# Queries and keys by halves of the heads in the first phase, and one plus the scale multiplied by GpSimd

## What is computed

```python
mod = (silu(c) @ wmod).reshape(2, 6, 1, 256)         # sa, ca, ga, sb, cb, gb
h  = layernorm(x) * (1 + ca) + sa                     # x: 2 x 2048 tokens x 256
xn = layernorm(h) * ln_g + ln_b
q, k, v = (xn @ W.T, in 8 heads of 32, for W in Wq, Wk, Wv)
def apply_rope(x):                                    # on q and k; x1, x2: a head's first and last 16
    return x * cos + concatenate([-x2, x1]) * sin
qp = einsum('bhtd,hd->bht', q[..., :3], head_dirs)    # and kp from k
```

## Time and profile before

| | us |
|---|---|
| Median of 3 runs | 2733.17 (2731.45 to 2739.83) |
| Profiled execution | 2730.83 |
| Its span, first to last instruction | 2729.1 |
| Part of the span in the changed phase | from about 23 to about 226 |

### The profile page before, as it was taken

One profiled execution on the slowest core, in us unless ns is written; L12 is line 12 of the kernel. 1 busy time (PEld: TensorE's weight loads), 2 busy tenths in 40 slices (PEclk: granted clock), 3 DMA queues, 4 the chain that ended last, 5 costly groups with the idle time before them and its releaser, 6 DMA issues. The chain is left out here.

```text
span 2729.1 us, 45326 instructions
## 1 busy us (share of the span) xinstructions
PE 2551.3 (93%) x14104; PEld 1541.0 (56%) x14104; DVE 2171.9 (80%) x4588; ACT 1589.6 (58%) x3509; POOL 554.8 (20%) x404
## 2 busy tenths in 40 slices
PE   7998999999999999996999999799989999997998
PEld 3444333333333333344777777578767777775877
DVE  5988999999999999975888888555658887885665
ACT  3443666666767766653666666544446666664442
POOL 1111011011100111035333333100033333331000
PEclk8997999999999999998999999999989999998999
DMA  3344354545445445453000000220020000001121
GB/s 131 118 133 125 102 133 114 131 122 149 115 110 130 121 126 135 128 177 106 16 17 15 21 16 15 64 89 22 2 63 9 8 9 8 10 16 43 46 68 40
DMA packets 124741, 204.95 MB, mean 75 GB/s; under 512 B 22736, under 2 KB 71952, under 8 KB 121280
## 3 DMA queue, kind: packets, MB, share of 16 engines
q1 hardware_dynamic: 111856, 170.39, 22.2%
q0 software_dynamic: 8688, 21.27, 2.8%
q10 hardware_dynamic: 4080, 11.86, 1.2%
HBM read 125.44 MB, written 54.13 MB: 66 GB/s over the span
## 5 line engine op out<-in xcount | busy, mean ns | idle before, releaser
L1084 ACT ACTIVATE probs<-st_ps 128x512 f32<-128x512 f32 (+3 forms) x640 | 339.0, 530 | 298.7 <-PE st_ps L1013 164.3
L1137 DVE SCALAR_TENSOR_TENSOR geo_x<-geo_rows,kp_t 128x512 f32<-128x512 f32 (+3 forms) x640 | 436.9, 706 | 3.8 <-ACT probs L1086 3.7
L1116 DVE TENSOR_REDUCE chunk_max<-a_ps 128x1 f32<-128x512 f32 (+3 forms) x640 | 358.6, 601 | 37.1 <-PE a_ps L996 31.7
L1086 ACT ACTIVATE probs<-geo_x 128x512 f32<-128x512 f32 (+3 forms) x640 | 360.7, 564 | 12.8 <-DVE geo_x L1143 12.8
L1417 PE MATMUL local_in_ps<-w_local,local_ht 128*128 128x512 f32 x1152 | 321.7, 416 | 9.4 <-ACT local_sq L1559 5.3
L1578 ACT ACTIVATE local_probs<-local_s_ps,local_bias,local_inv 128x256 f32<-128x256 f32 x512 | 282.6, 563 | 13.8 <-DVE local_bias L1673 13.8
L1585 ACT ACTIVATE local_pt<-local_pt_ps 128x512 f32<-128x512 f32 x256 | 152.3, 596 | 209.0 <-PE local_pt_ps L1475 200.7
L1028 PE MATMUL o_ps<-probs,vx_first 128*33 128x512 f32 (+3 forms) x1280 | 274.0, 550 | 0.0
L1856 PE MATMUL ff_ag_ps<-ff_ht_parts,w 128*128 128x512 f32 (+1 forms) x1056 | 255.4, 400 | 17.5 <-DVE ff_gate L1965 9.3
L1028 PE MATMUL o_ps<-probs,vx_ 128*33 128x512 f32 (+3 forms) x1280 | 270.3, 544 | 0.0
L1669 DVE TENSOR_REDUCE local_top<-local_s_ps 128x4 f32<-128x1024 f32 x128 | 156.7, 1224 | 120.9 <-PE local_s_ps L1461 120.9
(11 more groups left out here) (197 smaller groups left out, 4216.9 us busy)
## 6 DMA issues: line engine op xcount, KB each, us to landing
geo_rows<-geo SPq DMA_DIRECT2D x64, 512.0 KB, 7.6
piece_lo<-in_pieces POOLq DMA_DIRECT2D x15, 768.0 KB, 5.7
weight_parts<-piece_hi SPq DMA_DIRECT2D x15, 768.0 KB, 3.4
weight_parts<-piece_lo SPq DMA_DIRECT2D x15, 768.0 KB, 6.0
raw<-out_t SPq DMA_DIRECT2D x128, 64.0 KB
shares_in<-shares SPq DMA_DIRECT2D x64, 128.0 KB, 4.9
q_first<-q_parts SPq DMA_DIRECT2D x24, 256.0 KB, 4.1
k_first<-k_parts SPq DMA_DIRECT2D x24, 256.0 KB, 6.3
```

Of the source, the lines that this page charges most:

```text
L1084: act.activation(probs[:, s % PSLOTS, 0, off:GTOK], st_ps[:, (b * NB + s) % STBANKS, off:GTOK], ACT.Exp).then_inc(q["st_used"], 1)
L1086: act.activation(probs[:, s % PSLOTS, 1, off:GTOK], geo_x[:, s % GSLOTS, off:GTOK], ACT.Exp).then_inc(q["probs_ready"], 1)
L1116: dve.reduce_max(chunk_max[:, it, c:c + 1], a_ps[:, n % ABANKS, 0:width], AX.X).then_inc(q["a_used"], 1)
L1137: ins = dve.scalar_tensor_tensor(out[:, off:GTOK], geo[:, 1, at], kp_t[:, j, ds(b, 1)].rearrange("p o -> p o"), geo[:, 0, at], ALU.add, AL ...
```

## The change

In words, part by part:

- The weight columns of queries and of keys are ordered by halves of the heads: first the first 16 columns of all 8 heads (128 columns), then the last 16 of all. Both terms of the rotary sum then exist already, and the products with rotated columns go. `w_qkv` has 3 x 256 columns for 5 x 256.
- There are two units for four: queries and keys. A unit's `qk_ps[:, u, half, :]` holds both halves. `rot_c` is one instruction of 1024 columns with the cosine repeated, `rot_s` two of 512 with the halves exchanged (the sign now in the scale factor), the sum, `hi` and `lo` one of 1024 each.
- The three coordinates of a head's direction lie all in the first half, so that a product with the directions is one matmul for two.
- The product with one plus the scale moves from DVE to POOL, for groups 1 to 7; on DVE a wait for it is left. POOL does it behind its offset of the first norm and ahead of `second_scale`, and so ahead of the next fetch.
- The order on DVE becomes `rotate(n, 0)`, wait, `rotate(n, 1)`, `low_part(n, 0)`, `shifted(n + 1)`, `low_part(n, 1)`; that on ACT both `hi`, both values, `normed`.
- SP stores the queries as soon as their `lo` is there and the keys after theirs. A store now takes 16 rows of each of 8 heads, 8 x 16 x 512, where it took 128 successive rows.

The core of the diff:

```diff
@@ SP: send
-                    sp.wait_ge(q["hi_done"], 4 * n + 4 + START)
-                    sp.wait_ge(q["lo_done"], 4 * n + 4 + START)
                     for r, store in enumerate((S.q_parts, S.k_parts)):
+                        sp.wait_ge(q["hi_done"], 2 * n + r + 1 + START)
+                        sp.wait_ge(q["lo_done"], 2 * n + r + 1 + START)
                         for part, tile in enumerate((hi, lo)):
                             for k in range(CC):
-                                dst = store[part, ds(n // GPB * H + k * 4, 4), :, ds(n % GPB * GTOK, GTOK)]
-                                sp.dma_start(dst.rearrange("h d t -> (h d) t"), tile[:, r, k, :].bitcast(F32)).then_inc(q["parts_out"], 16)
+                                dst = store[part, ds(n // GPB * H, H), k * HD:(k + 1) * HD, ds(n % GPB * GTOK, GTOK)]
+                                sp.dma_start(dst, tile[:, r, k, :].bitcast(F32)).then_inc(q["parts_out"], 16)
@@ POOL: the loop over n
                     pool.tensor_tensor(offset[:, 0, :], centre[:, 0, :], rstd[:, 0, :], ALU.mult).then_inc(q["rstd1"], 1)
+                    pool.wait_ge(q["x_used"], n + 1 + START)
+                    pool.tensor_tensor(xhat[:, :, :], xhat[:, :, :], S.mod[:, 1, ds(n // GPB, 1), :].to_broadcast([P, GT, C]), ALU.mult).then_inc(q["chain1"], 1)
                     second_scale(n)
@@ ACT: group
-                    for u in range(4):
-                        if u == 3 and more:
-                            normed(n + 1)
-                        act.wait_ge(q["rope_done"], 4 * n + u + 1 + START)
+                    for u in range(2):
+                        act.wait_ge(q["rope_done"], 2 * n + u + 1 + START)
...
-                        act.activation(hi[:, u // 2, u % 2, :], qk[:, u // 2, u % 2, :], ACT.Copy).then_inc(q["hi_done"], 1)
+                        act.activation(hi[:, u, :, :], qk[:, u, :, :], ACT.Copy).then_inc(q["hi_done"], 1)
+                    for u in range(2):
+                        act.wait_ge(q["v_ready"], 2 * n + u + 1 + START)
+                        act.activation(S.v[:, ds(n * GT + 2 * u, 2), :, :],
+                                       v_ps[:, u, :].rearrange("p (t h d) -> p t h d", t=2, h=H), ACT.Copy).then_inc(q["v_used"], 1)
+                    if more:
+                        normed(n + 1)
@@ PE: group
-                    for u in range(4):
-                        pe.wait_ge(q["qk_used"], 4 * n + u + 1 + START)
-                        for rot in range(2):
-                            c0 = (u // 2 * 2 + rot) * C + u % 2 * P
+                    for u in range(2):
+                        pe.wait_ge(q["qk_used"], 2 * n + u + 1 + START)
+                        for half in range(2):
+                            c0 = u * C + half * P
...
-                        for k in range(CC):
-                            last = pe.matmul(dot_ps[:, :], (dirs_q if u == 0 else dirs)[:, k, :], qk[:, u, k, :],
-                                             start=k == 0, stop=k == CC - 1)
-                        last.then_inc(q["dot_ready"], 1)
+                        pe.matmul(dot_ps[:, :], (dirs_q if u == 0 else dirs)[:, :], qk[:, u, 0, :], start=True, stop=True).then_inc(q["dot_ready"], 1)
@@ DVE: modulated, rotate, group
                     if not scaled:
-                        dve.wait_ge(q["x_used"], n + 1 + START)
+                        dve.wait_ge(q["chain1"], n * LINKS + 3 + START)
+                        return
...
+                    dve.wait_ge(q["qk_ready"], 2 * n + u + 1 + START)
+                    dve.wait_ge(q["rope_done"], 2 * n + u + START)
+                    dve.scalar_tensor_tensor(rot_c[:, :, :], qk_ps[:, u, :, :], sc, cos[:, here].rearrange("p (o t) -> p o t", o=1).to_broadcast([P, 2, GTOK]), ALU.mult, ALU.mult)
+                    dve.scalar_tensor_tensor(rot_s[:, 0, :], qk_ps[:, u, 1, :], -sc, sin[:, here], ALU.mult, ALU.mult)
+                    last = dve.scalar_tensor_tensor(rot_s[:, 1, :], qk_ps[:, u, 0, :], sc, sin[:, here], ALU.mult, ALU.mult)
...
-                    for u, piece in enumerate((modulated, shifted, None, None)):
-                        rotate(n, u)
-                        if u:
-                            low_part(n, u - 1)
-                        if more and piece:
-                            piece(n + 1)
...
+                    rotate(n, 0)
+                    if more:
+                        modulated(n + 1)
+                    else:
+                        gates(2)
+                    rotate(n, 1)
+                    low_part(n, 0)
+                    if more:
+                        shifted(n + 1)
+                    low_part(n, 1)
```

More of the change, by code:

```diff
@@ L26 @@
 BH = B * H
+HD = D // 2
 EPS = 1e-5
@@ L123, in __init__ @@
         sb, _, sem = allocators(nc, ctx, S.sems)
-        self.w = sb("w_qkv", [P, CC, 5 * C])
+        self.w = sb("w_qkv", [P, CC, 3 * C])
         self.cos, self.sin = sb("cos_t", [P, T]), sb("sin_t", [P, T])
         self.ln_g, self.ln_b = sb("ln_g", [P, CC]), sb("ln_b", [P, CC])
-        self.dirs = sb("dirs", [P, CC, H])
+        self.dirs = sb("dirs", [P, H])
         self.xin, self.xhat = sb("xin", [P, GT, C]), sb("xhat", [P, GT, C])
@@ L205, in _ @@
                 c = Counter(dve, E.chain, base=0)
-                dve.memset(E.dirs[:, :, :], 0.0).then_inc(E.dirs_zero, 1)
+                dve.memset(E.dirs[:, :], 0.0).then_inc(E.dirs_zero, 1)
                 dve.wait_ge(stage_done, EXP_DONE)
@@ L396, in group @@
                     pe.wait_ge(q["xnt_ready"], CC * n + CC + START)
-                    for u in range(4):
-                        pe.wait_ge(q["qk_used"], 4 * n + u + 1 + START)
-                        for rot in range(2):
-                            c0 = (u // 2 * 2 + rot) * C + u % 2 * P
+                    for u in range(2):
+                        pe.wait_ge(q["qk_used"], 2 * n + u + 1 + START)
+                        for half in range(2):
+                            c0 = u * C + half * P
                             for k in range(CC):
-                                last = pe.matmul(qk_ps[:, u % 2, rot, :], w[:, k, c0:c0 + P], xnt[:, k, :],
+                                last = pe.matmul(qk_ps[:, u, half, :], w[:, k, c0:c0 + P], xnt[:, k, :],
                                                  start=k == 0, stop=k == CC - 1)
@@ L413, in group @@
                                 last = pe.matmul(v_ps[:, u, t * C:(t + 1) * C], xnt[:, k, (2 * u + t) * P:(2 * u + t + 1) * P],
-                                                 w[:, k, 4 * C:5 * C], start=k == 0, stop=k == CC - 1)
+                                                 w[:, k, 2 * C:3 * C], start=k == 0, stop=k == CC - 1)
                         last.then_inc(q["v_ready"], 1)
@@ L466, in rotate @@
                     here = ds(n % GPB * GTOK, GTOK)
-                    sc = 1.0 / math.sqrt(D) if u < 2 else 1.0
-                    dve.wait_ge(q["qk_ready"], 4 * n + u + 1 + START)
-                    dve.scalar_tensor_tensor(rot_c[:, u % 2, :], qk_ps[:, u % 2, 0, :], sc, cos[:, here], ALU.mult, ALU.mult)
-                    last = dve.scalar_tensor_tensor(rot_s[:, u % 2, :], qk_ps[:, u % 2, 1, :], sc, sin[:, here], ALU.mult, ALU.mult)
+                    sc = 1.0 / math.sqrt(D) if u == 0 else 1.0
+                    dve.wait_ge(q["qk_ready"], 2 * n + u + 1 + START)
[3 more added lines that the diff above has]
+                    last = dve.scalar_tensor_tensor(rot_s[:, 1, :], qk_ps[:, u, 0, :], sc, sin[:, here], ALU.mult, ALU.mult)
                     last.then_inc(q["qk_used"], 1)
-                    dve.wait_ge(q["qk_used"], 4 * n + u + 3 + START)
+                    dve.wait_ge(q["qk_used"], 2 * n + u + 3 + START)
                     if u == 0:
                         dve.wait_ge(q["dot_ready"], 2 * n + START)
-                    dve.tensor_tensor(qk[:, u // 2, u % 2, :], rot_c[:, u % 2, :], rot_s[:, u % 2, :], ALU.add).then_inc(q["rope_done"], 1)
+                    dve.tensor_tensor(qk[:, u, :, :], rot_c[:, :, :], rot_s[:, :, :], ALU.add).then_inc(q["rope_done"], 1)
                 def low_part(n, u):
-                    dve.wait_ge(q["hi_done"], 4 * n + u + 1 + START)
-                    dve.tensor_tensor(lo[:, u // 2, u % 2, :], qk[:, u // 2, u % 2, :], hi[:, u // 2, u % 2, :].bitcast(F32),
-                                      ALU.subtract).then_inc(q["lo_done"], 1)
+                    dve.wait_ge(q["hi_done"], 2 * n + u + 1 + START)
+                    dve.tensor_tensor(lo[:, u, :, :], qk[:, u, :, :], hi[:, u, :, :].bitcast(F32), ALU.subtract).then_inc(q["lo_done"], 1)
                 def directions(n, first):
@@ L512, in group @@
                         directions(n - 1, first)
-                    for u, piece in enumerate((modulated, shifted, None, None)):
-                        rotate(n, u)
-                        if u:
-                            low_part(n, u - 1)
-                        if more and piece:
```

(16 more changed lines are left out.)

12 lines of the change are left out of this document (4 added, 8 removed).

## The result

The changed kernel takes 2777.8 us in the median (2774.3 to 2785.7), the kernel before 2733.6 beside it: 1.016 times as long, 95% interval 1.0139 to 1.0177. The forecast was 2758, its range ended at 2775. The sign and the mechanism came as told, and the time outside the range.

The account below looks back on a forecast made before the run. PE and DVE were taken as near their limits, with the fetch of x behind `var2` a third limit. A cycle of 27.8 us for 23.03 gave +29.0, the end -2.3: +26.7 us, so 2758; range 2742 to 2775.

Parts of the forecast that it names:

- the end behind the last `lo`: End of the changed phase, from the last `lo` to the next block: 8.4 us, as before.
- the way from the last `var2` to the dot product: Last group: keys' dot product through power, `hn`, transposes, product and copy, some 7.5 us.
- The closed chain: Each group: x to `var2` 18.7 us, then `var2` through the fetch to the next x 9.1; cycle 27.8, before 23.03.
- (b): Behind `var2`: POOL's power slowed by DVE's subtraction with both inputs in SBUF, +0.95 us; bounds 0 and 1.2.
- (c): Between `var2` and x: the fetch shares transfer engines with 1 MB of stores, +1.7 us; bounds 0 and 3.5.
- The tail: From the seventh group's x to the next block: 51.3 us where it was 53.6, so -2.3.
- rival 1: Stores beginning with 8 run at half rate, about 182 GB/s: cycle 28.5, last stores 2.9 later, 2765 us; chance 0.25.
- rival 3: TensorE's clock stays low through the second unit too, some 2.5 us a group, +17: 2775 us; chance 0.08.
- The sum: Changed phase: first interval +5.1, five cycles of 27.8, seventh group +29.0, end -2.3; in all +26.7 us.
- Rival 4: x arrives early enough that DVE never waits; DVE's 19.7 to 21 bounds the cycle: about 2718 us, faster; chance 0.04.
- the lower bound: No POOL-DVE meeting and quiet queues: cycle 25.15, +10.7, 2742 us; chance 0.15 with what lies near it.
- hidden, with 1.5 us to spare: POOL's product ends some 6.8 us after x's statistics; DVE asks at 8.3, behind directions and a rotation.

Follow-up runs that it names:

- the early fetch: Changed kernel, but GpSimd issues the next fetch of x as soon as ScalarE has read x, no longer behind `var2`: 2767.2 us, 1.0122 of the kernel before.
- the second unit behind `var2`: Changed kernel, fetch untouched, but the second unit's rotation and the first subtraction stand behind `var2` again on DVE: 2754.9 us, 1.0082 of the kernel before.
- the kernel with all: Changed kernel with 16-first stores, fetch issued once x is read, second rotation and both subtractions behind `var2`, `hn` before keys' copy, product after directions: 2708.0 us, 0.9916.

## Why the mechanism was right and the size wrong

In one sentence: the chain was found, and three terms of the sum were too small, the fetch beside stores, the end behind the last `lo`, and the way from the last `var2` to the dot product.

*The closed chain*: right, in place and kind. Undoing the order alone returns half of the loss. The 18.7 from x to `var2` measured 18.6.

*(b), the meeting of subtraction and power*: right, the power takes 1.91 us for 1.01, and 1.01 again with the subtraction elsewhere.

*(c), the fetch beside stores*: here the first step failed. The forecast took 4.4 + 1.7 = 6.1 us. Measured: 4.5 where it is issued well ahead of the stores or behind them (the early fetch, and the second unit behind `var2`), 6.3 beside stores that begin with 16, 7.6 beside those of the changed kernel. The 1.7 was thus right for stores at the full rate, and the stores were not at it: the price of the pattern that begins with 8 was put on a rival, which had the right mechanism and 2.4 for (c), where it is 3.2. The stretches show a share of 0.5 at 181 to 205 GB/s, against 0.97 to 1.00 at 314 to 338 where only the order of the columns is changed. The Trainium skill, page "DMA: Bandwidth & Descriptors", section "Why a DMA increments its semaphore by 16 and not by 1", takes the largest number of engines up to 16 that divides the slowest dimension of both sides, so 8 for this pattern, and these traces agree. Rows of before could not speak for or against it; so the nearest row, stores that begin with 128, was no evidence against the rule, and 0.25 was too little for it.

*The tail*: the second step, and the larger for its size. Forecast 51.3 us from the seventh x to the next block, measured 57.5: +6.2. Two terms make it. The end behind the last `lo` was taken as before, 8.4, and measured 13.5 (253.93 to 267.43). With stores that begin with 16 it is 9.5 (246.44 to 255.93), so 4.0 of the 5.1 are the slower stores. The term of 7.5 from the last `var2` to the dot product measured 9.0 (228.41 to 237.43, the row with 7.89): the transposes took 1.97 us for the 1.1 taken, and the direction product 1.88 for 0.95, with the granted clock at 0.50 in that stretch. The other terms measured 0.4 less. Only rival 1 had a longer end of the phase, by 2.9. That is why the range broke: its lower end was made from (b) and (c) and its upper one, 2775, from rival 3's clock inside the groups, and neither let the tail grow.

*The sum*: the seventh x comes at 209.9 where 201.0 was said, +8.9 (2.1 up to the second x, 6.8 in five cycles), and the tail is +6.2; in all the phase is +41.8 where +26.7 was said. With 11.5 us for the pattern that begins with 8 the working gives +38. The median has 2 to 3 us more behind the phase, within what runs differ by. There is a slip as well: 2757.5 and the 2.3 by which the median lay higher give 2759.8 and not 2758. With the range moved up by the same 2 us its end is 2777, and 2777.8 is still outside.

*Rival 4, and the lower bound*: both wrong in a way that a result near the forecast would have hidden. Rival 4 has DVE's own work as the limit once x is early enough, and the lower bound has a cycle of 25.15. Neither holds: the keys' dot product is a second chain from `var2`, 9.15 us to the directions. By an estimate from the run with the early fetch it gives 28.15 less the hold of 2.5, 25.65, even with no wait for x. Its wait was in the rows, 0.68 us before the scan, and the prediction makes nothing of it; it said that this chain was about as tight as that of x. Behind it stands TensorE's first unit, the third.

*The product on GpSimd, "hidden, with 1.5 us to spare"*: true in the changed kernel. The product ends at 131.0 and DVE's second rotation, behind the wait for it, starts at 132.3. But it misses the directions by only 0.1 us, and only since x came late. Elsewhere it costs DVE 2.05 to 2.5 us when it meets an instruction of the directions, and 1.25 at a sum, both with two inputs in SBUF. The Trainium skill, page "SBUF — State Buffer", section "SBUF: two separate sides", has an exclusive lock of whole instructions for such a pair, kept by the one that starts first. The rows agree with whole instructions: the sum that starts 1.4 us before the product's end ends 1.1 us behind it. On who comes first they do not settle it: in the run with the early fetch the held row begins 0.26 us ahead of the product's (122.00, 122.26). Beside a rotation step that reads PSUM (1.21 us, 128.50 in the changed kernel) there is no hold.

*TensorE's clock*: the rival said a low clock would be hidden. It was 0.73 over five groups (1.00 in the earlier trace rows), and PE was busy for 16.6 us a group where 14 was said. DVE waited for no product of queries or keys but the first, so inside the groups it was hidden; it cost in the tail.

## What to carry to other kernels

When work is moved ahead of a signal, list everything that hangs on the signal, not only the next thing that waits: here a fetch, a dot product and TensorE's first unit each made a chain of 25.5 to 29 us. The early fetch alone won 7 us of the phase; the kernel with all, which has it and the rotation and the subtractions put back behind `var2`, left DVE no wait above 0.3 us in those groups. A wait of half a microsecond in an old profile marks such a chain as tight. If a change rearranges a tile, read the pattern of its stores: put a dimension of 16 or more first (16 and 128 ran at a share of about 1.0 here, 8 at 0.5), and forecast the time with the slow pattern as the likeliest when a written rule says so and no row speaks against it. Give GpSimd's products a place beside DVE instructions that read PSUM, by a wait if need be.

## What the runs showed of the hardware

Stores of 128 x 512 whose pattern in memory begins with 8 move 171 to 205 GB/s at a share of 0.47 to 0.53 in stretches of 2 us well inside them; with 16 first 314 to 338 at 0.97 to 1.00; with 128 first 364 at 1.03. The 512 KB fetch lands in 4.5, 6.3 or 7.6 us: with hardly a store beside it, with stores that begin with 16, with those that begin with 8. At the end of the phase SyncE takes 2.0, 3.0 and 2.5 us to issue the last three pairs of such stores, with 16 first 1.25, 1.2 and 1.9. The hold between GpSimd and DVE works both ways: a power of 1.0 us takes 1.9 to 2.0 beside a DVE subtraction or scan with two inputs in SBUF, and a DVE instruction of 0.68 us takes 2.7 to 3.2 beside a product of 2.4 to 2.6. A held sum of 1.22 us ends 1.08 to 1.10 us behind the product, whether it started 1.4 or 0.3 us before the product's end.
